# A fused attention, LoRA and LayerNorm kernel: v matrix ahead of q and k, row pieces ahead of weights, output slots in turn, bias by 32-row tiles

## What is computed

```python
q = einsum('bsD,Ddh->bsdh', x, Wq) + bq           # 32 heads of 128
k = (einsum('bsD,Ddh->bsdh', x, Wk) + bk)[..., 0]
v = (einsum('bsD,Ddh->bsdh', x, Wv) + bv)[..., 0]
scores = einsum('bsdh,bse->bsde', q, k) * scale    # sums over h: a 128x128 matrix per token
o = einsum('bsde,bse->bsd', softmax(scores), v)    # the same o for all 32 heads
x = layernorm(x + out)
base_out = einsum('btd,od->bto', x, base_W) + base_b
w = top-8 of softmax(x @ router_W + router_b), through expert_map
lora = einsum('bter,eor->bto', (x @ A) * w, B) * SCALING
x = layernorm(x + base_out + lora)
```

## Time and profile before

| what | value |
|---|---|
| time, median of 3 runs | 1363.35 us (1361.82 to 1365.39) |
| the profiled execution | 1368.05 us |
| its span, slowest core (core 2) | 1366.5 us |
| spans of the 8 cores | 1353.1 to 1366.5 us |
| TensorE (PE) busy | 1216.6 us, 89% |
| VectorE (DVE) busy | 780.8 us, 57% |
| ScalarE (ACT) busy | 548.2 us, 40% |
| GpSimd (POOL) busy | 161.1 us, 12% |

### The profile page before, as it was taken

How to read it: one execution, slowest core, us unless ns; L and a number is a source line. 1 busy time by engine, 2 the same in 40 slices (tenths; PEclk the granted TensorE clock), 3 DMA queues, 4 the chain that set the end, 5 groups by cost and what they waited for, 6 DMA issues and landing times.

```text
span 1366.5 us, 29162 instructions; the slowest of 8 cores (1353.1 to 1366.5 us)
## 1 busy us (share of the span) xinstructions
PE 1216.6 (89%) x10752; PEld 961.4 (70%) x10768; DVE 780.8 (57%) x1502; ACT 548.2 (40%) x856; POOL 161.1 (12%) x323
## 2 busy tenths in 40 slices
PE   2199799999999779999799697999999999699995
PEld 1088588888888757677566475676788798467774
DVE  2240045677845944348858578587788751255554
ACT  0011011111111026578577485787711111467776
POOL 4000011101111212301112011111110000000000
PEclk9999999999999979999989899899999999889998
DMA  9899999999999999936644656445447035468787
GB/s 119 78 161 163 171 175 170 147 167 160 172 167 170 167 151 141 146 65 93 108 83 70 117 93 114 71 79 104 80 87 130 8 68 137 138 203 264 260 250 254
DMA packets 96860, 187.86 MB, mean 137 GB/s; under 512 B 15824, under 2 KB 46800, under 8 KB 94416
## 3 DMA queue, kind: packets, MB, share of 16 engines
q0 software_dynamic: 44160, 122.82, 58.7%
q1 hardware_dynamic: 52560, 63.17, 15.7%
HBM read 260.52 MB, written 48.24 MB: 226 GB/s over the span
## 4 chain that ended last, share of the span: by engine, by line
PE 47%; DMA 18%; DVE 14%; another core or an unknown queue 8%; issue 8%; ACT 2%; POOL 1%; DVEq 0%; ACTq 0%; POOLq 0%; SPq 0%
PE pF L509 29%; DMA wqs<-wq 12%; DVE wqk L881 4%; PE pS L565 4%; DMA xw<-xr 4%; DVE wr L845 3%; PE pS L591 3%; PE pN L612 2%; DVE xT L1032 2%; PE pN L574 2%; DMA w<-wt 2%; PE pS L650 1%; PE pS L550 1%; PE pS L548 1%
## 5 line engine op out<-in xcount | busy, mean ns | idle before, releaser
L509 PE MATMUL pF<-w,xT 128*128 128x256 bf16 x8192 | 945.6, 276 | 68.5 <-DMA w<-wt 59.1
L509 PEld LDWEIGHTS pF<-w,xT 128*128 128x128 bf16 x8192 | 798.6, 99 | 203.3 <-issue 102.5
L729 ACT ACTIVATE p<-pS 128x1024 bf16<-128x1024 f32 x256 | 248.0, 1021 | 83.5 <-PE pS L591 83.5
L698 ACT ACTIVATE zo<-pF 128x256 bf16<-128x256 f32 x224 | 86.2, 385 | 454.7 <-PE pF L509 454.7
L881 DVE TENSOR_REDUCE wqk<-wqs 128x64 bf16<-128x2048 bf16 x64 | 144.0, 2279 | 178.2 <-DMA wqs<-wq 178.2
L845 DVE TENSOR_REDUCE wr<-w 128x64 bf16<-128x2048 bf16 x52 | 189.6, 3656 | 20.2 <-DMA w<-wt 19.7
L997 DVE SCALAR_TENSOR_TENSOR xr<-xr,ob 128x1024 bf16<-128x1024 bf16 x64 | 76.4, 1223 | 11.0 <-DMA xr<-xr 10.5
L591 PE MATMUL pS<-qx,kx 32*128 32x512 bf16 x512 | 53.4, 391 | 31.2 <-ACT p L729 31.2
L804 ACT ACTIVATE jk<-zu 128x2048 bf16<-128x2048 bf16 x32 | 61.1, 1910 | 42.2 <-DVE zu L1112 28.2
L565 PE MATMUL pS<-wqk,xT 128*128 128x257 bf16 x512 | 60.5, 281 | 16.3 <-DVE wqk L881 16.3
L311 POOL DMA_DIRECT2D w<-wt x64 | 34.1, 546 | 306.5 <-PE pF L509 187.3
(11 more groups left out here) (121 smaller groups left out, 735.2 us busy)
## 6 DMA issues: line engine op xcount, KB each, us to landing
w<-wt POOLq DMA_DIRECT2D x64, 512.0 KB, 13.8
wqs<-wq POOLq DMA_DIRECT2D x64, 512.0 KB, 11.4
y<-y SPq DMA_DIRECT2D x64, 512.0 KB, 6.3
xT<-xt POOLq DMA_DIRECT2D x16, 1024.0 KB, 104.6
xr<-xr POOLq DMA_DIRECT2D x64, 256.0 KB, 5.6
z<-zo SPq DMA_DIRECT2D x224, 64.0 KB, 7.4
zu<-z SPq DMA_DIRECT2D x48, 256.0 KB, 6.2
xs<-xr POOLq DMA_DIRECT2D x40, 256.0 KB, 5.8
```

The source lines that it names most:

```text
L509: ins = te.matmul(pF[k % 2][:, 0:HW], xT[:, t, c, :], W[h % 2][:, c, :], start=(i == 0), stop=(close and i == NCH - 1))
L698: s_ge.inc(sc.activation(m[f"zo{k % n}"], pF[k % 2][:, 0:HW], AF.Copy))
L729: s_ex.inc(sc.activation(m[f"p{Q % 2 * 2 + half}"], pS[half], AF.Exp, scale=SCALE_Q))
```

## The change

The diff, cut to its core:

```diff
+    scr_s = dram("scr_s", [NT], F32, "Internal")
-              *[(f"dg{i}", 128, BF16) for i in range(4)], ...
+              ("sdr", 512, BF16), ...
-        yp = []
+        yp, prior = [], []
         for t in range(T):
+            at_ = [t, t, t - 2, t - 2] if t >= 2 else [0, 0, 1, 1]
             ...
+            if t == 0:
+                prior.append([None] * 4)
+            elif t == 1:
+                prior.append([0, 1, 2, 3])
+            else:
+                first = {2: 4, 3: 6}.get(t, 4 * t - 8)
+                prior.append([None, None, first, first + 1])
+        vbank = [pN[0], pN[1], pS[0][:, 512:1024], pS[1][:, 512:1024]]
...
 # GpSimd, attention, tile a
-                    if a in SQ_TILES:
+                    if a in SQ_TILES and a - 1 not in W_TILE:
                         row_xw(n)
...
                     if a in W_TILE:
+                        if a + 1 in SQ_TILES:
+                            row_xw(n + 2)
                         load_w(W_TILE[a])
...
 # GpSimd, ahead of the last pass
                 load_w(14)
+                def load_sdr(i):
+                    if i >= 2:
+                        g.wait_ge(s_c.h, 2 * NPAIR * (i - 1))
+                    s_sdr[i % 2].inc(g.dma_start(
+                        m["sdr"][:, i % 2 * 256:i % 2 * 256 + 256],
+                        scr_s[i * 256:i * 256 + 256].unsqueeze(0).to_broadcast([128, 256])), 16)
+                g.wait_ge(s_scs.h, 16)
+                load_sdr(0)
+                load_sdr(1)
                 load_w(15)
+                for i in range(2, T // 2):
+                    load_sdr(i)
...
 # SyncE, ahead of the first loads of z
+                sy.wait_ge(s_s32.h, 1)
+                s_scs.inc(sy.dma_start(scr_s.rearrange("(t p) -> p t", t=T), m["std32"],
+                                       allow_slow_non_contiguous=True), 16)
...
 # TensorE, last pass
+                def bias(t, prs):
+                    if t == 0:
+                        te.wait_ge(s_b8.h, 16)
+                    if prs[0] == 0 and t % 2 == 0:
+                        te.wait_ge(s_sdr[t // 2 % 2].h, 16 * (t // 4 + 1))
+                    for pr in prs:
+                        i = NPAIR * t + pr
+                        if i >= NCB:
+                            te.wait_ge(s_cu.h, i - NCB + 1)
+                        r = slice(pr % 4 * 32, pr % 4 * 32 + 32)
+                        te.matmul(cbank(i), m["sdr"][r, t % 4 * 128:t % 4 * 128 + 128],
+                                  m["brow"][r, pr * 512:pr * 512 + 512], start=True, stop=False)
-                    ins = te.matmul(cbank(i), m[f"dg{t % 4}"], m["brow"][:, at_:at_ + 512],
-                                    start=False, stop=True)
...
-                        for i in range(NPAIR * of[0], NPAIR * of[0] + NPAIR):
-                            corr(i)
+                        for prs in (range(4), range(4, NPAIR)):
+                            bias(of[0], prs)
+                            for pr in prs:
+                                corr(NPAIR * of[0] + pr)
...
 # ScalarE
-                for t in range(T):
-                    for _ in range(SQ_QKV[t]):
-                        square(nsq)
-                        nsq += 1
-                    if t % 4 == 3: ...
+                for gq in range(4):
+                    sc.wait_ge(s_vq.h, gq + 1)
+                    if gq == 0:
+                        sc.wait_ge(s_wqr.h, NQP)
+                    s_ve.inc(sc.activation(vT[:, gq * 512:gq * 512 + 512], vbank[gq],
+                                           AF.Identity, bias=m["bvc"]))
+                for i in range(NSQQ):
+                    square(i)
-                        if q == 2:
-                            r_y.landed(sc, 4 * (t - 2 if t >= 2 else t))
+                        if prior[t][q] is not None:
+                            r_y.landed(sc, prior[t][q])
+                        if (t, q) == (0, 2):
+                            sc.wait_ge(s_gd.h, UIDX[(15, 1)] - NEV + 1)
...
 # VectorE, ahead of the router
+                s_s32.inc(v.tensor_scalar(out=m["std32"], in0=m["std"], scalar1=1.0 / 32,
+                                          scalar2=None, op0=ALU.mult))
```

More of the change, by code:

```diff
@@ L218, in build_program @@
         place(regR, ("zu0", D, BF16), ("zu1", D, BF16), ("brow", D, BF16), ("jk", 2048, BF16),
-              *[(f"dg{i}", 128, BF16) for i in range(4)], ("su0", 9, F32), ("su1", 9, F32), ("sq20", 2, F32), ("sq21", 2, F32),
+              ("sdr", 512, BF16), ("su0", 9, F32), ("su1", 9, F32), ("sq20", 2, F32), ("sq21", 2, F32),
               ("fcols", 10, F32))
@@ L567, in _ @@
                     s_q.inc(ins)
-                    if t % 4 == 3:
-                        gq = t // 4
-                        bank = pN[gq % 2]
-                        if gq >= 2:
-                            te.wait_ge(s_ve.h, gq - 1)
-                        for c in range(NCH):
-                            ins = te.matmul(bank.rearrange("p (t n) -> p t n", t=4),
-                                            wv[:, c, :], xT[:, 4 * gq:4 * gq + 4, c, :],
-                                            start=(c == 0), stop=(c == NCH - 1))
-                        s_vq.inc(ins)
                 def scores(Q):
@@ L587, in scores @@
                         te.wait_ge(s_qe.h, T)
+                        te.wait_ge(s_ve.h, 4)
                     for r in range(4):
@@ L713, in _ @@
                 sc.wait_ge(s_bv.h, 16)
-                for t in range(T):
-                    for _ in range(SQ_QKV[t]):
-                        square(nsq)
-                        nsq += 1
-                    if t % 4 == 3:
-                        gq = t // 4
-                        sc.wait_ge(s_vq.h, gq + 1)
-                        s_ve.inc(sc.activation(vT[:, gq * 512:gq * 512 + 512], pN[gq % 2],
-                                               AF.Identity, bias=m["bvc"]))
+                for gq in range(4):
+                    sc.wait_ge(s_vq.h, gq + 1)
[5 more added lines that the diff above has]
+                    square(i)
+                nsq = NSQQ
                 sc.wait_ge(s_sq.h, NSQQ)
@@ L806, in square_z @@
                         accum_out=m[f"sq2{t % 2}"][:, half:half + 1]))
-                sc.wait_ge(s_std.h, 2)
-                sc.wait_ge(s_hw.h, T)
-                sc.wait_ge(s_rs.h, 4 * T)
-                for t in range(3):
-                    deviations(t)
                 for t in range(T):
-                    if t + 3 < T:
-                        deviations(t + 3)
                     square_z(t, 0)
@@ L1142, in last_quarter @@
                     v.wait_ge(s_n2.h, t + 1)
-                    r_y.landed(v, 4 * (t - 2 if t >= 2 else t) + 1)
+                    if prior[t][3] is not None:
+                        r_y.landed(v, prior[t][3])
                     s_yv.inc(v.tensor_scalar(out=yp[t][3], in0=m[f"zu{t % 2}"][:, 3072:4096],
```

37 lines of the change are left out of this document (13 added, 24 removed).

## The result

The changed kernel takes 1341.36 us (median of 4 runs, 1338.2 to 1375.25), the kernel before on the same chip 1363.38 (4 runs, 1361.82 to 1365.39). The ratio is 0.983, 95% interval 0.982 to 0.985: 22 us faster, where 59 were forecast, and outside the range. (In the execution of 1375.25 the cores of one die ran at a lower clock; the ratio is made without it.) The slowest core is now core 1.

A forecast was written before the change was run, and what follows sets the result against it. TensorE, busy 89% of the slowest core's span, could gain from idle stretches or fewer matmuls: v 3, row piece 35, slots 11, bias 10, together 59 us off 1363.35, giving 1304; forecast 1298 to 1311 (chance 0.5), range 1291 to 1327.

The forecast's parts named there:

- The three waits: TensorE idle through late row pieces in attention, stores of y in the last pass, and VectorE's sums before q and k.
- I put the last square at 571: Stage 2, v ahead of q and k: ScalarE's last square comes 1.4 us earlier; 3 us gained (0.5 to 5.5).
- The bound of 568.5: Stage 2: earliest time for the last square, if three waits of a us behind v each cost the stream.
- ScalarE waits 1.1 us, TensorE less or a little more: Attention: second square's row piece is barely late behind the weights, 1.3 us for each of three tiles; 35 us gained.
- rival A: Attention: second square waits in all three tiles as the queue drains slowly; 1318 us halfway, 1333 at the bound; chance 0.2.
- The rate of 158 GB/s: Attention: rate read from 664 to 686, at which 3.41 MB up to the second square's piece take 21.6 us.
- The 39 us to be had: Attention: three TensorE stalls of 13.0 us each, behind late row pieces for the first square, would go.
- The slots, 11 us: Last pass: waits for stores of y go, so 11 us gained up to unit (14, 3), 8 to 12.5.
- all 8.3 us of VectorE's second wait: Last pass: quarter 3 of tile 1 follows at once if tile 0's stores have landed, removing 8.3 us.
- The bias, 0.85 a tile: Last pass: two 32-row groups of 0.33 us replace seven matmuls of 1.51; 10 us over tiles 3 to 14.
- The new transfers are hidden: Before the last pass: the store of 2048 deviations, issued 21 us ahead, and its small loads cost nothing.
- rival C: Before the last pass: deviations' store is priced per element, TensorE stands, slower than before, up to 1719 us; chance 0.04.

The follow-up runs named there:

- Run 12: Changed kernel with the store of deviations issued earlier, weights in halves, 34 squares in stage 2 and some of them between the copies of v: 1306.37 us, ratio 0.963.
- run 8: Changed kernel with 34 instead of 40 squares ahead of the scores, the other six in attention tiles 13 to 15: 1332.42 us, ratio 0.982.
- run 2: Kernel before with only the row piece put ahead of the weights: 1334.22 us, ratio 0.981.
- run 7: Changed kernel with the weights after tiles 3, 6 and 9 in two halves, the second behind the second square's row piece: 1321.79 us, ratio 0.975.
- run 3: Kernel before with only the slots of y taken in turn: 1354.20 us, ratio 0.995.
- run 4: Kernel before with only the bias done by 32-row matmul groups from stored and reloaded deviations: 1361.47 us, ratio 1.000.
- run 6: Changed kernel with the store of 2048 deviations issued 13 units earlier, among the last stores of z: 1337.92 us, ratio 0.975.

## Why the prediction was wrong

**What bounds the kernel**: right. The three waits are where the time was. Run 12 is 49.5 us faster than the kernel before on its chip (48.7 on the mean of the spans), six squares moved included, which the forecast did not have. Its stretches sum to 62 us less than in the trace of the kernel before, but that trace is of another chip, where that kernel is slower, so of the stretches' differences (stage 2 -9.8, attention -34.4, the two last ones -9.0 and -6.6) a part is the chip. Most of the gain forecast was there; the change as made did not get it.

**v, "I put the last square at 571"**: this step failed. -3 us was forecast, +3.1 found; on core 1 the last square began at 574.35, 105 us after the units instead of 99.8. The bound of 568.5 took it for granted that ScalarE saves what it waited behind v between squares; in fact all four copies now stand ahead of the first square, which begins 28.4 us after the units instead of 26.8, and nothing is caught up, because the stream takes 1.8 to 2.0 us a piece in every kernel. Counted from the sums the stage got 4.3 us longer (97.5 against 93.2). That the stream, not TensorE, sets the end was in the prediction, and run 8 shows its price with v ahead: six squares fewer, 11 to 12 us. What was missing is the conclusion that v ahead of the first square can then only lose.

**The row piece, "ScalarE waits 1.1 us, TensorE less or a little more"**: the term was mis-sized, -35 forecast, -23.8 found. The stalls of 13 us vanished. What stayed is rival A, "the second square waits", at 11 us instead of its 14. The rate of 158 GB/s was taken over a stretch in which three smaller transfers shared the engines, and of a chain of 24 us the difference to the time when the piece is wanted was 1.1. On core 1 the same 3.41 MB, from the issue at 667.26 to the landing, took 27.0 us, 126 GB/s, and the square wanted them after 22.2. The landing took 16 to 18.5 us after issue in tile 4, and 13.1 were free; on the chip of run 2 it took 12 to 16 over all three tiles, and waits of at most 2.9 us were left. The 39 us to be had were also read from core 2, one of the worst: attention without a stall takes 374.0 us in run 7, so before it 36.9 were to be had on the mean of the cores. A term that hangs on such a margin should have been priced between its two sides, not at one. The price of a late piece also held more than the wait, since TensorE's turn waits for VectorE there. Run 7 removes it: no wait over 0.4 us is left at P = 5.

**The slots, 11 us**: the mechanism was right and the size off; alone it measured 8.6 us (run 3). The sum took it that quarter 3 of tile 1 follows at once, so that all 8.3 us of VectorE's second wait go; 3.0 of them stayed on the mean of the cores, because the stores of tile 0 had not landed. In the changed kernel 5.3 of them were hidden by the late `sdr` and the late weights.

**The bias, 0.85 a tile**: a size was off. The group of four took 0.33 us, as the scores of the earlier trace rows showed, but each group also starts 0.09 us late, and that of three takes 0.37; so 0.60 a tile was saved. The late start could have been read in the kernel before, on core 2:

```profile
675.34 0.40 PE L612 MATMUL pN<-p,vm 128*32 128x512 bf16 x4
```

It comes 2.29 us after the 20 matmuls at 673.05 begin, and 20 of them take 2.18 (32 take 3.49). The prediction read its 0.33 us from the start of the scores, and so without it. What makes the 0.09 is not shown; the rule of the Trainium skill that a change of mode drains TensorE (TensorEngine Tiling (Array Packing), Key Properties) agrees with it, and has no size. Twelve tiles make 7 us instead of 10, and 5.6 to 6.9 came in run 4. In the changed kernel 4.8 came, because single tiles took longer, with VectorE waiting for z and TensorE for VectorE: the forecast had a DMA share of 0.88, and from 1200 to 1300 us it was 0.93 to 0.98 over the cores.

**"The new transfers are hidden"**: this step failed, at 9 us (run 6: 3.9 ahead of the first correction, 5.3 behind it). The choice between price by element and price by crowd was put as 435 us or a few; it was 12 to 18.5 for 2048 elements, 6 to 9 ns each. That is less than the 21 us assumed as cover, but the store is not the end of the chain: `load_sdr` waits for it and took 11.10 us more on core 1, 29 together. And behind the store stood the loads of z, behind `sdr` the weights of block 15. It is rival C in small. The page of the profile counts the packets, here of the changed kernel and of run 2, which has no such store:

```profile
DMA packets 100076, 188.40 MB, mean 141 GB/s; under 512 B 18016, under 2 KB 50016, under 8 KB 97632
```

```profile
DMA packets 96860, 187.86 MB, mean 141 GB/s; under 512 B 15824, under 2 KB 46800, under 8 KB 94416
```

2192 more are under 512 bytes, 2048 of which the elements would make, so each travelled by itself. The rule in the Trainium skill (DMA: Bandwidth & Descriptors, Rules for kernel authors) that such a pattern lowers to one descriptor per element agrees with that, and the trace adds the price. Run 6 takes the cost away by moving one issue.

Of the 37 us missing on the median the means of the cores show 34: 6 in stage 2, 11 in attention, 5 ahead of the last pass, 7 in its first tiles, 5 at its end. Not settled is why the same load lands faster on one chip than on another, and why z came late in single tiles of the last pass. From TensorE's last matmul to the end it takes 15.2 us instead of 14.1, but from its last unit only 0.4 more, as forecast for tile 15.

## What to carry to other kernels

When a stall of a transfer is removed by moving it ahead of a big one, look at the next small transfer that now stands behind the big one, and cut the big one in two rather than reorder alone. Price a stream (pieces times their period) before the order of the engines around it: with 40 squares of 1.9 us v ahead of q and k bought nothing, with 34 it shortened the stage by 5 us, and 34 without v ahead bought 1. And follow a new tiny transfer through every queue that it enters: what counted was not its bytes but what was issued behind it.

## What the runs showed of the hardware

- A store of 2048 elements of 4 bytes from 128 partitions took 12.2 to 18.5 us to land, and the eight loads issued behind it on the same queue took 14 to 21 us to issue instead of 4.3 to 5.7.
- A 256 KB load behind 2 MB of weights on one queue landed, in tile 4, after 16.1 to 18.5 us on one chip (changed kernel), 12.9 to 15.9 on another (run 2) and 15.0 to 18.4 on a third (run 8); behind 1 MB after 7.8 to 12.6 on that third one (run 7).
- A group of 32-row matmuls of 512 columns behind a 128-row one began 0.09 us late; to the next kind four took 0.33 us and three 0.37.
- The slowest core stood 12.0 us above the mean span with waits that fell on the cores unevenly (run 8), and 5.7 without them (run 7); 13.2 in run 2, where the sums over `wq` came unevenly.
- The same kernel took 1315 us on one chip and 1306 on another, and the kernel before 1355.88 to 1370.33 on three: comparisons of a few us hold on one chip only.
